# Key and query products of a graph-attention layer: one fp32 product each replaced by three products of rounded high and low parts

## The chip, the cores and the metric

One NeuronCore of one Trainium2 chip runs the whole program in one launch. The metric is device time in microseconds (us) of that launch, lower is better. Beside it stands one execution taken by the hardware profiler; its rows are in us from the start of its span unless marked ns. TensorE's matmuls are PE in the rows and its weight loads PEld; VectorE is DVE, ScalarE ACT, GpSimd POOL, and SP is the engine that only issues DMAs.

## The reference

Two graph layers over 16 batches of 512 nodes with 128 features. The change lies in the second layer; what comes before it is cut.

```python
x = x + _L0_gnn_ref(relu(layernorm(x)), adj, ...)      # eight Euler steps over the graph
h = relu(layernorm(x))
# _L1_gnn_ref, 4 heads of 32:
x1 = relu(layernorm((L_norm @ h) @ Wc + bc) * g1 + be1) + h
q, k, v = x1 @ Wq, x1 @ Wk, x1 @ Wv                     # [512, 128] each, per batch
scores = q @ k.T / sqrt(32), masked by adj > 0
o = softmax(scores) @ v
x2 = layernorm(x1 + o @ Wo + bo) * g2 + be2
out = x + layernorm(x2 + gelu(x2 @ W1 + b1) @ W2 + b2) * g3 + be3
```

## The kernel before

Layer 0 runs up to 419 us; it also takes batch 0 of layer 1 as far as its queries and keys, with helpers of its own calls that the change leaves as they are. Then a block boundary, at which all engines meet, and layer 1.

Layer 1 is written as rounds `r`, unrolled, the same list for every engine. In round `r` batch `r` enters (x1, its turned form x1T, keys, queries, values), batch `r - 1` is attended (scores, softmax, turned probabilities, products with v), and batch `r - 2` leaves (normalisation by the sums, output projection, second layer norm). Batches 1 to 15 enter in rounds 1 to 15. A round has 16 units `u` (4 tiles of 128 query rows by 4 heads). In each unit every engine does its share of the attention and then what the constants `AT_...` put in that unit. Every engine works through its own list strictly in the order of the code; semaphores alone tie the lists together, and an instruction that waits holds up all behind it on its engine.

The share of unit `u` of the batch attended:

- TensorE: `turn` (four 128x128 transposes of an older unit's probabilities, L1767), `scores` of unit `u + 1` (one product of 512 columns, L1754), and in odd units `values` (16 small products, L1787).
- VectorE: the mask and the row minimum of unit `u` (L1935), called mask u below; it writes `prob`. For units 0, 7, 11, 13, 15 it also copies turned probabilities out of PSUM (L1922), three units later.
- ScalarE: the exponential of unit `u` with its sum (L1873), called exp u below, which waits for mask u; the other eleven copies (L1862), also three units later.

What stands around the change in round `r`:

- u = 1, VectorE: `residual` (L340) writes x1 of batch `r`. It waits for `z_norm` (L331) of GpSimd, which was started in the round before.
- u = 2, TensorE: `x1_transpose` (L347) puts x1 turned in PSUM bank 4 (`A_BANK`). ScalarE: `x1T_out` (L354) copies it to `x1T` in SBUF, behind exp 2. VectorE: mask 2, then the copy of unit 15 of the batch before.
- u = 3, TensorE: `k_product` (L359), one fp32 product of 512 columns, which the trace shows as two matmul instructions. ScalarE: `k_hi_out` (L377) writes the rounded high part of k, behind exp 3. VectorE: mask 3, the copy of unit 0, then statistics of the batch that leaves (L285, L291).
- u = 4, TensorE: `q_product` (L363) into bank 4. ScalarE: exp 4, the copy of unit 1, `q_hi_out` (L384), `spread` (L1899). VectorE: mask 4, `k_lo_out` (L389).
- u = 5, VectorE: mask 5, `q_lo_out` (L395), then the standardisation of the batch that leaves (`z_std`, L308).
- u = 6 to 9, TensorE: the graph product of batch `r + 1`, three float32r products a unit (L1829); it waits for `q_lo_ready`, since it uses bank 4 too.
- u = 12, VectorE: `z2` (L1972). GpSimd's `x_bo` (L1711) waits for it, and behind `x_bo` in GpSimd's list stand `rstd_b` (L212), `z_gain` (L327) and `z_norm` (L331) of batch `r + 1`.
- u = 14, TensorE: `v_product` (L368) from `x1T`.

High and low parts: a float32r tile holds a rounded value, the high part is the rounded copy, the low part is the difference to it. The helper `products` pairs high with high, high with low and low with high:

```python
    (left_hi, left_lo), (right_hi, right_lo) = left, right
    return (left_hi, right_hi), (left_hi, right_lo), (left_lo, right_hi)
```

The mask and the exponential in the code:

```python
dve.tensor_tensor_reduce(prob[u % RING][:, :], psum[u % 2][:, :], mask[:, u // HEADS, :], ...).then_inc(masked, 1)
act.wait_ge(masked, UNITS * a + u + 1)
```

Of the kernel before, what the change touches and what calls it, by code (L numbers as in the profile page):

```python
# [18 lines left out]
F32 = mybir.dt.float32  # L19
F32R = mybir.dt.float32r  # L20
BF16 = mybir.dt.bfloat16
ALU = mybir.AluOpType
# [82 lines left out]
def two_layers(nc, x, adj, alpha, w, d, fc_w, fc_b, Wc, bc, g1, be1, Wq, Wk, Wv, Wo, bo, g2, be2, W1, b1, W2, b2,  # L105
# [4 lines left out]
    with ExitStack() as whole:  # L110
# [19 lines left out]
        two_over_lam = tensor(whole, "two_over_lam", [P, 1])  # L130

        one = Shared()
        one.row_in = tensor(whole, "row_in", [1, ROWS, D])
        one.bc_all = tensor(whole, "bc_all", [P, ROWS, D])
        one.Wcs = tensor(whole, "W_c", [P, D])
        one.Wqs = tensor(whole, "W_q", [P, D])
# [11 lines left out]
        one.mean_rstd = tensor(whole, "mean_rstd_a", [P, NT])  # L148
        one.shift = [tensor(whole, f"shift_a{i}", [P, NT]) for i in range(2)]
        one.h = [tensor(whole, f"h{i}", [P, NT, D]) for i in range(2)]  # L150
        one.y, one.Lnorm, one.ident, one.exponent = y, adjT, ident, exponent
        one.dve_waited, one.pool_waited = waited
        one.L_lo = L_lo
# [1258 lines left out]

AT_X1, AT_X1T, AT_X1T_OUT, AT_K, AT_Q, AT_K_HI, AT_Q_HI, AT_K_LO, AT_Q_LO = 1, 2, 2, 3, 4, 3, 4, 4, 5
AT_V, AT_V_OUT = 14, 14
AT_CONV, AT_CONV_OUT, AT_Z, AT_Z_OUT, AT_Z_MOMENTS, AT_Z_STD = 6, 9, 10, 11, 12, 14
AT_Y_MOMENTS, AT_H = 9, (11, 12, 13)
# [24 lines left out]
def layer1(nc, whole, tensor, sem, psum, one, out_dram, y, mask, ident, exponent, waited):  # L1443
# [164 lines left out]
    with ExitStack() as ctx:  # L1608
        def sb(name, shape, dt=F32):
# [2 lines left out]
        stats_c, mv_c = sb("stats_c", [P, NT, 6]), sb("mv_c", [P, NT, 2])  # L1612
        ve_c, rstd_c = sb("ve_c", [P, NT]), sb("rstd_c", [P, NT])
        z2_std = sb("z2_std", [P, NT, D])
        one.x1[1], one.v[1] = sb("x1_1", [P, NT, D]), sb("v_1", [P, NT, D])
        x1 = one.x1
        x1_bo = [sb(f"x1_bo{i}", [P, NT, D]) for i in range(2)]
# [12 lines left out]
        L_parts = (sb("L_hi", [P, NT, N], F32R), one.L_lo)  # L1630
        h_parts = tuple(sb(f"h_{part}", [P, NT, D], F32R) for part in ("hi", "lo"))

        L_hi_ready, L_lo_ready, h_hi_ready, h_lo_ready = (
            sem(n) for n in ("L_hi_ready", "L_lo_ready", "h_hi_ready", "h_lo_ready"))
        z2_std_ready, z2_gain_ready, sums_inv_ready = (
# [40 lines left out]
        with nc.Block() as block:  # L1676
# [12 lines left out]
            def _(pool):  # L1689
# [24 lines left out]
                def round_(r, s, half):  # L1714
                    enters, attends, leaves = parts(r)
                    if leaves:
                        spread_inverses(r - 2)
                    if within(r, 1, BATCH - 2):
                        split_h(r + 1, 1 - s)
                    e = r - 3  # L1720
                    if within(r, 3, BATCH + 2):
                        inverse_root(pool, e, mv_c, c_mv, ve_c, rstd_c, c_pool, z2_std_ready, e, exponent, pool_waited)

                        pool.wait_ge(z2_std_ready, e + 1)
                        pool.tensor_tensor(out=z2_gain[:, :, :], in0=z2_std[:, :, :], in1=all_tiles(one, G2),
                                           op=ALU.mult).then_inc(z2_gain_ready, 1)
                        pool.wait_ge(z2_gain_ready, e + 1)
                        pool.tensor_tensor(out=x2[:, bass.ds(e * N, N)].rearrange("p (t d) -> p t d", d=D),
                                           in0=z2_gain[:, :, :], in1=all_tiles(one, BE2), op=ALU.add
                                           ).then_inc(x2_ready, 1)  # L1730
                    if within(r, 0, BATCH - 3):
                        h_scales(pool, one, r + 2, s)
                    if enters:
                        add_bo(r, s)
                    if within(r, 0, BATCH - 2):
                        z_root(pool, one, r + 1)
                    if within(r, 0, BATCH - 2):
                        norm_z(pool, one, r + 1)
                add_bo(0, 0)
                unrolled(round_, BATCH + 2, first=1)  # L1740
                scales_3(pool, 0)
# [5 lines left out]
            def _(pe):  # L1747
                def scores(a, s, u, half):
                    if u == 0:

                        pe.wait_ge(stacked[s], STACK_DMAS * half)
                    at_least(pe, masked, UNITS * a + u - 1)
                    t, head = divmod(u, HEADS)
                    pe.matmul(psum[u % 2][:, :], q_stack[s][:, head, t * P:(t + 1) * P], k_stack[s][:, head, :],  # L1754
                              start=True, stop=True).then_inc(scores_psum, 1)

                def turn(batch, u):

# [34 lines left out]
                def round_(r, s, half):  # L1793
                    enters, attends, leaves = parts(r)
                    a, e = r - 1, r - 2
                    for u in range(UNITS):
# [19 lines left out]
                            last.then_inc(spread_psum, 1)  # L1816
                        if u == AT_K and enters:
                            at_least(pe, oT_ready, r - 2)
                            k_product(pe, one, psum[7 - s], r)
                        if u == AT_Q and enters:  # L1820
                            q_product(pe, one, A_BANK, r)
                        if AT_CONV <= u < AT_CONV + NT and within(r, 0, BATCH - 2):
                            if u == AT_CONV:
                                pe.wait_ge(q_lo_ready, r + 1)
# [34 lines left out]
            def _(act):  # L1859
# [5 lines left out]
                def round_(r, s, half):  # L1865
                    enters, attends, leaves = parts(r)
                    a, e = r - 1, r - 2
                    for u in range(UNITS):
# [10 lines left out]
                        if x not in DVE_COPIES:  # L1879
                            if u < TURN_LAG and leaves:  # L1880
                                copy_turned(e, x)
                            if u >= TURN_LAG and attends:
                                copy_turned(a, x)
                        if u == AT_X1T_OUT and enters:
                            x1T_out(act, one, A_BANK, r)
                        if u == AT_K_HI and enters:
                            k_hi_out(act, one, psum[7 - s], r, s, half)
# [31 lines left out]
            def _(dve):  # L1919
# [5 lines left out]
                def round_(r, s, half):  # L1925
# [3 lines left out]
                    for u in range(UNITS):  # L1929
# [22 lines left out]
                        if u == AT_RINV and leaves:  # L1952
                            dve.wait_ge(exp_done, UNITS * (e + 1))
                            at_least(dve, rinv_ready, e)
                            dve.reciprocal(sums_inv[:, :], row_sums[s][:, :]).then_inc(sums_inv_ready, 1)
                        if u == AT_K_LO and enters:
                            k_lo_out(dve, one, psum[7 - s], r)
                        if u == AT_Q_LO and enters:
# [70 lines left out]
```

## Time and profile before

| what | value |
|---|---|
| median of 3 runs | 921.42 us (921.39, 921.42, 926.23) |
| profiled execution, its own time | 925.83 us |
| its span, first to last instruction | 924.0 us |
| PE busy | 871.8 us, 94% of the span |
| DVE busy | 650.8 us, 70% |
| ACT busy | 540.9 us, 59% |
| POOL busy | 324.8 us, 35% |
| mean granted TensorE clock | 0.979 |

Matmuls are pipelined and their ends are modelled, so a busy share of PE is not a share of its peak; the distance from one start to the next tells more. Layer 1 with its 15 rounds takes from 419 us to about 812 us; the profiled execution is 4.41 us longer than the median of the three runs.

### The profile page before, as it was taken

How to read it: one execution, taken by the hardware profiler on the slowest of the kernel's cores; microseconds unless marked ns; L12 is line 12 of the kernel's file. 1: busy time of each engine (PE TensorE's matmuls, PEld its weight loads, DVE VectorE, ACT ScalarE, POOL GpSimd, SP SyncE). 2: the span in 40 equal slices, each digit the busy share in tenths (PEclk: the TensorE clock that was granted, in tenths of full speed). 3: DMA queues.
4: the chain of work that ended last, by engine and by line, in shares of the span. 5: the costliest groups of instructions: out<-in, count | busy, mean ns of one | idle time of the engine just before them, and what ended most of it. 6: DMA issues, size and time to landing. Idle time of an engine off the chain costs nothing.

```text
span 924.0 us, 19065 instructions
## 1 busy us (share of the span) xinstructions
PE 871.8 (94%) x6765; PEld 712.7 (77%) x6765; DVE 650.8 (70%) x2110; ACT 540.9 (59%) x1234; POOL 324.8 (35%) x426
## 2 busy tenths in 40 slices
PE   6999999999999999988999999999999999889993
PEld 5779989899999888975777777777777777667772
DVE  6856464644454456536898988888898988887786
ACT  3144342433333323216988888888888887885674
POOL 4111111102020304202354554455555553224776
PEclk9799999999999899999999999999999999999998
DMA  3000000000000000503444455554444545500222
GB/s 100 0 12 13 12 12 12 12 13 12 12 24 1 23 12 1 137 1 105 126 109 98 116 138 139 138 138 111 112 104 106 121 138 138 138 2 1 59 57 69
DMA packets 46428, 61.73 MB, mean 67 GB/s; under 512 B 3567, under 2 KB 21246, under 8 KB 46334
## 3 DMA queue, kind: packets, MB, share of 16 engines
q1 hardware_dynamic: 46034, 60.38, 25.3%
q8 instruction: 55, 0.90, 0.4%
q14 instruction: 39, 0.32, 0.1%
q10 hardware_dynamic: 300, 0.13, 0.1%
HBM read 39.53 MB, written 20.97 MB: 65 GB/s over the span
## 4 chain that ended last, share of the span: by engine, by line
DVE 15%; PE 12%; issue 10%; POOL 9%; ACT 8%; DVEq 0%; POOLq 0%; ACTq 0%
DVE prob L1935 5%; PE bank L1767 4%; PE bank L1787 3%; ACT prob L1873 3%; PE bank L1829 2%; POOL z_gain L327 2%; POOL z_norm L331 2%; ACT probT L1862 2%; DVE z_std L308 2%; POOL x_bo L1711 2%; POOL rstd_b L212 1%; DVE probT L1922 1%; PE bank L1754 1%; POOL rstd L212 1%; DVE stats_c L285 1%
## 5 line engine op out<-in xcount | busy, mean ns | idle before, releaser
L1873 ACT ACTIVATE prob<-prob,low 128x512 f32<-128x512 f32 x256 | 184.0, 719 | 62.9 <-DVE low L1935 61.0
L1935 DVE CUSTOM_DVE_ANT_0 prob<-bank,mask 128x512 f32<-128x512 f32 x256 | 171.0, 682 | 24.2 <-PE bank L1754 22.6
L1767 PE MATMUL bank<-ident,prob 128*128 128x128 f32 x1024 | 161.7, 281 | 13.5 <-ACT probT L1862 13.5
L1767 PEld LDWEIGHTS bank<-ident,prob 128*128 128x128 f32 x1024 | 113.3, 141 | 59.9 <-issue 35.7
L1754 PE MATMUL bank<-k_stack,q_stack 128*128 128x512 f32 x256 | 123.3, 482 | 2.5 <-DVE low L1935 1.4
L820 PE MATMUL bank<-B_hi,halves 128*128 128x384 f32 x384 | 106.4, 339 | 1.6 <-DVE halves L1183 1.1
L1862 ACT ACTIVATE probT<-bank 128x512 f32<-128x512 f32 x176 | 102.6, 583 | 2.6 <-PE bank L1767 1.1
L791 PE MATMUL bank<-halves,P3T_hi 128*128 128x256 f32 x512 | 98.8, 295 | 3.4 <-DVE halves L1201 2.2
L791 PEld LDWEIGHTS bank<-halves,P3T_hi 128*128 128x128 f32 x512 | 84.6, 201 | 5.8 <-DVE halves L1201 2.5
L610 POOL TENSOR_SCALAR var_eps<-mv 128x4 f32<-128x4 f32 x16 | 3.6, 228 | 242.2 <-DVE mv L1127 242.2
L1787 PE MATMUL bank<-probT,v 128*32 128x128 f32 x2048 | 82.3, 279 | 2.7 <-ACT probT L1862 1.1
L1787 PEld LDWEIGHTS bank<-probT,v 128*32 128x32 f32 x2048 | 48.2, 109 | 43.0 <-issue 32.2
L791 PE MATMUL bank<-halves,P3T_lo 128*128 128x256 f32 x256 | 74.6, 291 | 0.0
L820 PEld LDWEIGHTS bank<-B_hi,halves 128*128 128x128 f32 x384 | 70.1, 188 | 4.5 <-DVE halves L1183 2.0
L973 ACT ACTIVATE Sq<-bank,trace_inv 128x512 fp32r<-128x512 f32 x44 | 30.2, 687 | 61.8 <-PE bank L775 61.8
L820 PE MATMUL bank<-B_lo,halves 128*128 128x384 f32 x192 | 64.6, 336 | 0.0
L1922 DVE COPY probT<-bank 128x512 f32<-128x512 f32 x80 | 55.0, 687 | 10.2 <-PE bank L1767 9.5
L964 ACT ACTIVATE halves<-bank 128x512 fp32r<-128x512 f32 x48 | 28.5, 593 | 51.0 <-PE bank L783 51.0
L1193 DVE TENSOR_TENSOR y<-bank,y 128x128 f32<-128x128 f32 x64 | 18.5, 289 | 56.2 <-PE bank L820 46.9
L1183 DVE TENSOR_TENSOR halves<-bank,halves 128x512 fp32r<-128x512 f32 x48 | 33.0, 688 | 33.9 <-ACT halves L964 33.9
L1754 PEld LDWEIGHTS bank<-k_stack,q_stack 128*128 128x128 f32 x256 | 48.7, 191 | 6.9 <-DVE low L1935 5.5
L791 PEld LDWEIGHTS bank<-halves,P3T_lo 128*128 128x128 f32 x256 | 51.4, 201 | 0.0
(263 smaller groups left out, 1963.3 us busy)
## 6 DMA issues: line engine op xcount, KB each, us to landing
k_stack<-bounce_q SPq DMA_DIRECT2D x64, 256.0 KB, 4.8
q_stack<-bounce_k SPq DMA_DIRECT2D x64, 256.0 KB, 7.5
bounce_q<-k_parts SPq DMA_DIRECT2D x16, 512.0 KB, 2.8
bounce_k<-q_parts SPq DMA_DIRECT2D x16, 512.0 KB, 3.1
x_in<-in_x_dram SPq DMA_DIRECT2D x16, 256.0 KB, 2.7
out_dram<-probT SPq DMA_DIRECT2D x16, 256.0 KB, 2.3
y<-in_adj_dram SPq DMA_DIRECT2D x4, 256.0 KB, 3.4
W1s<-in_L_gnn_W_dram SPq DMA_DIRECT2D x1, 128.0 KB, 2.2
```

Source lines behind the costliest of these rows:

```text
L791: last = pe.matmul(psum[2 + nt // 2][:, nt % 2 * 2 * D:(nt % 2 + 1) * 2 * D], power[:, k, nt * P:(nt + 1) * P], c[:, k, :, :].rearrange("p ...
L820: last = pe.matmul(psum[nt % 2][:, 0:GROUP * D], x[:, nt * P:(nt + 1) * P], c[:, m, :, :].rearrange("p i d -> p (i d)"), start=m == 0 and ...
L964: act.activation(T_parts[m][0], psum[4 + m][:, :], ACT.Copy).then_inc(T_hi_ready[m], 1)
L973: act.activation(Sq[1 - s][:, mt, :], SQ_BANK[:, :], ACT.Identity, scale=trace_inv2[:, 0:1], accum_out=v[:, mt:mt + 1]).then_inc(square_re ...
L1183: dve.tensor_tensor(out=T_parts[m][1], in0=psum[4 + m][:, :], in1=T_parts[m][0].bitcast(F32), op=ALU.subtract).then_inc(T_lo_ready[m], 1)
L1754: pe.matmul(psum[u % 2][:, :], q_stack[s][:, head, t * P:(t + 1) * P], k_stack[s][:, head, :], start=True, stop=True).then_inc(scores_psum, 1)
L1767: last = pe.transpose(psum[2 + u % 2][:, mt * P:(mt + 1) * P], prob[u % RING][:, mt * P:(mt + 1) * P], ident[:, :])
L1787: last = pe.matmul(psum[6 + s][rows, t * P:(t + 1) * P], v[s][:, mt, rows], probT[(HEADS * t + head) % TURNED][:, mt, :], start=mt == 0, s ...
L1862: act.activation(probT[u % TURNED][:, :, :].rearrange("p t n -> p (t n)"), psum[2 + u % 2][:, :], ACT.Copy).then_inc(copied_act, 1)
L1873: act.activation(prob[u % RING][:, :], prob[u % RING][:, :], ACT.Exp, bias=low[:, u % TURNED:u % TURNED + 1], scale=-1.0, accum_out=row_su ...
L1922: dve.tensor_copy(probT[u % TURNED][:, :, :].rearrange("p t n -> p (t n)"), psum[2 + u % 2][:, :]).then_inc(copied_dve, 1)
L1935: dve.tensor_tensor_reduce(prob[u % RING][:, :], psum[u % 2][:, :], mask[:, u // HEADS, :], 1.0, 3e38, ALU.add, ALU.min, low[:, u % TURNED ...
```

## The change

The fp32 key and query products of batches 1 to 15 become three float32r products each. At the start of layer 1 GpSimd splits W_k and W_q into high and low parts (four instructions on 128x128). In each round ScalarE writes the high part of x1T in unit 2, into the tile of `q_parts`, which is free by then; VectorE writes the low part in unit 2 (`AT_X1T_LO = 2`), behind the copy of that unit; ScalarE makes the fp32 copy `x1T`, which the value product still reads, in unit 3, once the low part is done. TensorE's key product waits for the low part, and its query product for the fp32 copy, since it writes the bank that both read. A loading buffer, `row_in`, moves into a part of `y` that is not used yet at that time.

```diff
--- before.py
+++ after.py
@@ -130,7 +130,6 @@
         two_over_lam = tensor(whole, "two_over_lam", [P, 1])
 
         one = Shared()
-        one.row_in = tensor(whole, "row_in", [1, ROWS, D])
         one.bc_all = tensor(whole, "bc_all", [P, ROWS, D])
         one.Wcs = tensor(whole, "W_c", [P, D])
         one.Wqs = tensor(whole, "W_q", [P, D])
@@ -148,6 +147,7 @@
         one.mean_rstd = tensor(whole, "mean_rstd_a", [P, NT])
         one.shift = [tensor(whole, f"shift_a{i}", [P, NT]) for i in range(2)]
         one.h = [tensor(whole, f"h{i}", [P, NT, D]) for i in range(2)]
+        one.row_in = y[0:1, 12 * N:12 * N + ROWS * D].rearrange("o (r d) -> o r d", d=D)
         one.y, one.Lnorm, one.ident, one.exponent = y, adjT, ident, exponent
         one.dve_waited, one.pool_waited = waited
         one.L_lo = L_lo
@@ -1412,7 +1412,7 @@
 
 
 
-AT_X1, AT_X1T, AT_X1T_OUT, AT_K, AT_Q, AT_K_HI, AT_Q_HI, AT_K_LO, AT_Q_LO = 1, 2, 2, 3, 4, 3, 4, 4, 5
+AT_X1, AT_X1T, AT_X1T_OUT, AT_X1T_LO, AT_K, AT_Q, AT_K_HI, AT_Q_HI, AT_K_LO, AT_Q_LO = 1, 2, 2, 2, 3, 4, 3, 4, 4, 5
 AT_V, AT_V_OUT = 14, 14
 AT_CONV, AT_CONV_OUT, AT_Z, AT_Z_OUT, AT_Z_MOMENTS, AT_Z_STD = 6, 9, 10, 11, 12, 14
 AT_Y_MOMENTS, AT_H = 9, (11, 12, 13)
@@ -1612,6 +1612,8 @@
         stats_c, mv_c = sb("stats_c", [P, NT, 6]), sb("mv_c", [P, NT, 2])
         ve_c, rstd_c = sb("ve_c", [P, NT]), sb("rstd_c", [P, NT])
         z2_std = sb("z2_std", [P, NT, D])
+        x1T_parts = tuple(one.q_parts[:, part, :] for part in range(2))
+        Wk_parts, Wq_parts = (tuple(sb(f"{n}_{part}", [P, D], F32R) for part in ("hi", "lo")) for n in ("W_k", "W_q"))
         one.x1[1], one.v[1] = sb("x1_1", [P, NT, D]), sb("v_1", [P, NT, D])
         x1 = one.x1
         x1_bo = [sb(f"x1_bo{i}", [P, NT, D]) for i in range(2)]
@@ -1630,6 +1632,7 @@
         L_parts = (sb("L_hi", [P, NT, N], F32R), one.L_lo)
         h_parts = tuple(sb(f"h_{part}", [P, NT, D], F32R) for part in ("hi", "lo"))
 
+        x1T_hi_ready, x1T_lo_ready, W_split = sem("x1T_hi_ready"), sem("x1T_lo_ready"), sem("W_split")
         L_hi_ready, L_lo_ready, h_hi_ready, h_lo_ready = (
             sem(n) for n in ("L_hi_ready", "L_lo_ready", "h_hi_ready", "h_lo_ready"))
         z2_std_ready, z2_gain_ready, sums_inv_ready = (
@@ -1736,6 +1739,12 @@
                         z_root(pool, one, r + 1)
                     if within(r, 0, BATCH - 2):
                         norm_z(pool, one, r + 1)
+                pool.wait_ge(one.weights_loaded, 16 * 5)
+                for n, (source, (hi, lo)) in enumerate(((one.Wks, Wk_parts), (one.Wqs, Wq_parts))):
+                    pool.tensor_copy(hi[:, :], source[:, :]).then_inc(W_split, 1)
+                    pool.wait_ge(W_split, 2 * n + 1)
+                    pool.tensor_tensor(out=lo[:, :], in0=source[:, :], in1=hi[:, :].bitcast(F32),
+                                       op=ALU.subtract).then_inc(W_split, 1)
                 add_bo(0, 0)
                 unrolled(round_, BATCH + 2, first=1)
                 scales_3(pool, 0)
@@ -1753,6 +1762,11 @@
                     t, head = divmod(u, HEADS)
                     pe.matmul(psum[u % 2][:, :], q_stack[s][:, head, t * P:(t + 1) * P], k_stack[s][:, head, :],
                               start=True, stop=True).then_inc(scores_psum, 1)
+
+                def split_product(pe, bank, parts):
+                    for n, (w, x) in enumerate(products(parts, x1T_parts)):
+                        last = pe.matmul(bank[:, :], w[:, :], x, start=n == 0, stop=n == 2)
+                    return last
 
                 def turn(batch, u):
 
@@ -1816,9 +1830,12 @@
                             last.then_inc(spread_psum, 1)
                         if u == AT_K and enters:
                             at_least(pe, oT_ready, r - 2)
-                            k_product(pe, one, psum[7 - s], r)
+                            pe.wait_ge(W_split, 4)
+                            pe.wait_ge(x1T_lo_ready, r)
+                            split_product(pe, psum[7 - s], Wk_parts).then_inc(one.k_psum, 1)
                         if u == AT_Q and enters:
-                            q_product(pe, one, A_BANK, r)
+                            pe.wait_ge(x1T_ready, r + 1)
+                            split_product(pe, A_BANK, Wq_parts).then_inc(one.q_psum, 1)
                         if AT_CONV <= u < AT_CONV + NT and within(r, 0, BATCH - 2):
                             if u == AT_CONV:
                                 pe.wait_ge(q_lo_ready, r + 1)
@@ -1882,6 +1899,11 @@
                             if u >= TURN_LAG and attends:
                                 copy_turned(a, x)
                         if u == AT_X1T_OUT and enters:
+                            act.wait_ge(one.x1T_psum, r + 1)
+                            act.wait_ge(one.q_written[1 - s], 16 * (half + s))
+                            act.activation(x1T_parts[0], A_BANK[:, :], ACT.Copy).then_inc(x1T_hi_ready, 1)
+                        if u == AT_K_HI and enters:
+                            act.wait_ge(x1T_lo_ready, r)
                             x1T_out(act, one, A_BANK, r)
                         if u == AT_K_HI and enters:
                             k_hi_out(act, one, psum[7 - s], r, s, half)
@@ -1953,6 +1975,11 @@
                             dve.wait_ge(exp_done, UNITS * (e + 1))
                             at_least(dve, rinv_ready, e)
                             dve.reciprocal(sums_inv[:, :], row_sums[s][:, :]).then_inc(sums_inv_ready, 1)
+                        if u == AT_X1T_LO and enters:
+                            dve.wait_ge(x1T_hi_ready, r)
+                            dve.tensor_tensor(out=x1T_parts[1], in0=A_BANK[:, :],
+                                              in1=x1T_parts[0].bitcast(F32), op=ALU.subtract
+                                              ).then_inc(x1T_lo_ready, 1)
                         if u == AT_K_LO and enters:
                             k_lo_out(dve, one, psum[7 - s], r)
                         if u == AT_Q_LO and enters:
```

## Rows read from the trace of the kernel before

**Rows 1.** The page, part 1: busy us, share of the span, instructions.
```profile
PE 871.8 (94%) x6765; PEld 712.7 (77%) x6765; DVE 650.8 (70%) x2110; ACT 540.9 (59%) x1234; POOL 324.8 (35%) x426
```

**Rows 2.** Busy us by window, one round: length, PE, PEld, DVE, ACT, POOL; clock.
```profile
604.00:630.00 26.00, 25.20 (x256) 18.67 (x256) 23.07 (x77) 22.06 (x54) 13.37 (x17) 1.00 0.49 123
```

**Rows 3.** Chain of waits through round 8: start, us, what was last.
```profile
603.77 0.29 DVE x L340
...
610.44 0.59 ACT q_parts L384
...
611.67 1.11 DVE z_std L308 x4
...
622.19 0.70 DVE z L1972
...
629.88 0.30 DVE x L340
```

**Rows 4.** Timeline of VectorE, units 2 to 9 of that round.
```profile
605.37 0.68 DVE L1922 COPY probT<-bank 128x512 f32<-128x512 f32 x1
...
605.97 0.67 DVE L1935 CUSTOM_DVE_ANT_0 prob<-bank,mask 128x512 f32<-128x512 f32 x1
...
608.51 0.69 DVE L1935 CUSTOM_DVE_ANT_0 prob<-bank,mask 128x512 f32<-128x512 f32 x1
...
609.13 0.69 DVE L389 TENSOR_TENSOR k_parts<-bank,k_parts 128x512 fp32r<-128x512 f32 x1
...
609.73 0.68 DVE L1935 CUSTOM_DVE_ANT_0 prob<-bank,mask 128x512 f32<-128x512 f32 x1
...
611.06 0.69 DVE L395 SCALAR_TENSOR_TENSOR q_parts<-bank,q_parts 128x512 fp32r<-128x512 f32 x1 [0.64 <-ACT q_parts L384]
...
616.45 0.69 DVE L1935 CUSTOM_DVE_ANT_0 prob<-bank,mask 128x512 f32<-128x512 f32 x1 [1.00 <-PE bank L1754]
```

**Rows 5.** Timeline of ScalarE, units 2 to 4 of that round.
```profile
605.48 0.72 ACT L1873 ACTIVATE prob<-prob,low 128x512 f32<-128x512 f32 x1 [0.24 <-DVE low L1935]
...
606.20 0.58 ACT L354 ACTIVATE x1T<-bank 128x512 f32<-128x512 f32 x1
...
608.06 0.60 ACT L377 ACTIVATE k_parts<-bank 128x512 fp32r<-128x512 f32 x1 [0.55 <-PE bank L359]
...
609.24 0.72 ACT L1873 ACTIVATE prob<-prob,low 128x512 f32<-128x512 f32 x1 [0.59 <-DVE low L1935]
```

**Rows 6.** Timeline of TensorE, units 3 to 6 of that round.
```profile
606.92 1.10 PE L359 MATMUL bank<-x1T,W_k 128*128 128x512 f32 x2
...
607.95 0.64 PE L1787 MATMUL bank<-probT,v 128*32 128x128 f32 x16
...
609.26 1.02 PE L363 MATMUL bank<-x1T,W_q 128*128 128x512 f32 x2
...
610.11 0.60 PE L1767 MATMUL bank<-ident,prob 128*128 128x128 f32 x4
...
612.19 0.39 PE L1829 MATMUL bank<-L_hi,h_hi 128*128 128x512 f32 x1
...
612.42 0.40 PE L1829 MATMUL bank<-L_lo,h_hi 128*128 128x512 f32 x1
```

**Rows 7.** Timeline at the start of layer 1, round 1.
```profile
419.71 1.28 POOL L1711 TENSOR_TENSOR x_bo<-x,bc_all 128x512 f32<-128x512 f32 x1 [34.15 <-POOLq L564]
...
421.63 1.62 POOL L1696 TENSOR_TENSOR h_lo<-h,h_hi 128x512 fp32r<-128x512 f32 x1
...
425.38 1.12 PE L359 MATMUL bank<-x1T,W_k 128*128 128x512 f32 x2 [0.84 <-ACT x1T L354]
...
426.39 0.68 DVE L1935 CUSTOM_DVE_ANT_0 prob<-bank,mask 128x512 f32<-128x512 f32 x1
...
430.89 0.50 PE L1829 MATMUL bank<-L_hi,h_hi 128*128 128x512 f32 x1 [0.26 <-DVE q_parts L395]
```

**Rows 8.** Chain of waits in round 2.
```profile
450.64 1.06 PE bank L359 x2
```

## The prediction

> **What bounds the kernel now.** I read the page first, then the busy time of one round, then the chain of waits, and last the timeline of that round around the change. The page makes TensorE look like the bound, busy 94% of the span [rows 1], and in a round it is 25.20 of 26.00 us [rows 2]. But its matmuls overlap each other in the records, and the weight loads fill only 18.67 us. VectorE is busy 23.07 us and ScalarE 22.06 [rows 2]. No engine is full, so the order of the work decides, and that is what the chain of waits shows [rows 3].
>
> Follow round 8. It starts with `residual` on VectorE at 603.77, runs over `q_hi` on ScalarE at 610.44 and `z_std` at 611.67 to z2 at 622.19, then through GpSimd's list to z_norm, and the next residual starts at 629.88 [rows 3]: 26.11 us, the length of a round. The chain is a loop, since the residual of a round needs z_norm from the round before, and GpSimd makes that only after z2. What is lost between residual and z2 on the chain lengthens every round.
>
> The change acts in units 2 to 5, and there the reader should look at VectorE [rows 4]. The copy of unit 2 starts at 605.37, mask 3 at 605.97, mask 4 at 608.51, `k_lo` at 609.13, mask 5 at 609.73; none of them has a wait in its row, VectorE goes through its list without a pause. The one wait is that of `q_lo` for ScalarE, 0.64 us. Yet that wait hangs on VectorE too: ScalarE's exp 4 waited 0.59 us for mask 4 [rows 5], and behind exp 4 stand the copy of unit 1 and `q_hi`. So mask 3, mask 4, exp 4, `q_hi`, `q_lo`, `z_std` form one string that starts when mask 3 starts. TensorE stands beside it: behind the key product it goes on at 607.95 [rows 6], and nobody on the string waits for that.
>
> **The change, part by part.**
>
> *The products.* TensorE spends 1.03 us on the key product (606.92 to 607.95) and 0.85 on the query product (609.26 to 610.11) [rows 6]. The three float32r products of 512 columns in unit 6 follow each other by 0.23 us (612.19, 612.42) [rows 6], so each triple takes 0.69. The change removes 0.34 + 0.16 = 0.50 us a round on TensorE. In rounds 3 to 15 I count this as nothing, since TensorE is not on the string there; were it, it would be 15 x 0.50 = 7.5 us.
>
> *The high part.* It takes the place of the old copy, same engine, same bank, same shape: 606.20 to 606.78 [rows 5]. It can't start earlier, because it is behind exp 2, which starts at 605.48 after mask 2 [rows 5]. Cost nothing.
>
> *The low part.* One VectorE instruction like `k_lo`: 0.69 us from PSUM and SBUF [rows 4], and the next starts 0.60 after its start (609.13 to 609.73). It stands in unit 2 ahead of mask 3, and it waits for the high part. VectorE is done with its copy at 606.05 and then holds until 606.78. A VectorE instruction starts about 0.03 after the ScalarE one it waits for (`q_lo` at 611.06 [rows 4], behind a `q_hi` from 610.44 to 611.03 [rows 3]), so the low part starts at 606.81 and mask 3 at 607.41 instead of 605.97 [rows 4]: 1.44 us later, of which 0.60 is work and 0.84 is the wait. Queued behind the low part are mask 3, the copy of unit 0, the statistics, mask 4; waiting for these are exp 3 and exp 4, then the string above. It has no slack, so I take the whole 1.44 a round. The lower bound is 0.60, the work alone, if the wait were recovered further on.
>
> *The fp32 copy in unit 3.* One more ScalarE copy of 0.58 [rows 5], behind exp 3 and ahead of `k_hi` and exp 4. Exp 3 now follows mask 3 at about 608.1 and is over by 609.0; the copy then ends at 609.5, `k_hi` at 610.0. Mask 4 is now at 608.51 + 1.44 = 609.95, so exp 4 comes at 609.24 + 1.44 = 610.68 at the earliest. About 0.7 us cover is left, so the copy costs nothing in rounds 3 to 15; without that cover it would cost up to 0.58.
>
> *The new waits on TensorE.* The key product waits for the low part, until 607.5 instead of starting at 606.92 [rows 6], and is over at 608.2; the products with v behind it come 0.3 later than 607.95, turned tiles too. The query product waits for the fp32 copy, 609.5 against 609.26. Both shifts are smaller than the 1.44 of the string, so they don't set it.
>
> *Splitting the weights.* Four GpSimd instructions of 128x128 at the head of its list. The row nearest to them is a 128x512 addition, 1.28 us [rows 7]; a quarter of it each is 1.3 us, whole ones would be 5.1. Behind them stand x_bo of batch 0 and the parts of h, whose last one ends at 423.25; the graph product needs these at 430.89, and the key product of round 1 starts at 425.38 [rows 7]. Even 5.1 us from 419.71 ends at 424.8. Cost nothing. The moved loading buffer adds no transfer and no wait: nothing.
>
> *Rounds 1 and 2* differ. In round 1 VectorE comes late to mask 3 (426.39) anyway, for another splitting; the low part finds its high part ready and pushes mask 3 by 0.60 only. ScalarE is late there too, and the fp32 copy adds up to 0.58 to `q_hi`, so the graph product at 430.89 [rows 7] comes about 1.1 later (0.6 to 1.4). In round 2 the key product itself is on the chain [rows 8]: it starts some 0.65 later (0.69 + 0.03 less what it waited already), the triples give 0.50 back, and the fp32 copy of 0.58 comes ahead of a ScalarE that has no slack in this round; I take 0.6 (0.2 to 1.4).
>
> *Sum.* 13 rounds x 1.44 = 18.7, plus 1.1 and 0.6: 20.4 us. The profiled execution would go from 925.83 to 946.2. It is 4.41 us above the median of the three runs; the addition is the same for both, so the median goes from 921.42 to 941.8, I say **942**.
>
> One reading of the page decides whether TensorE's saving counts at all. By its busy share in the round, 25.20 us, it would be the bound, and the sum would be -7.5 us; by VectorE's 23.07 of 26.00 the change adds to the fullest engine [rows 2]. The Trainium skill's page Perfetto Trace Analysis, section Identifying the Most-Contended Engine, says that the busy share of matmuls is a poor measure since they are pipelined, that weight loads are a better one, and that occupancy is fair for VectorE. By that rule VectorE is the most contended engine and this change loads it further, which speaks against it; the trace agrees with the order (18.67 against 23.07).
>
> **The rivals.**
>
> *Only VectorE's own work counts.* The 0.84 us of waiting come back, because VectorE idles further on: mask 9 waits 1.00 us for TensorE at 616.45 [rows 4]. Then 15 x 0.60 = 9.0, 930.4 us. For it: 2.9 us of idle VectorE in the round. Against it: the scores that mask 9 waits for hang on exp 6 and a copy behind `z_std`, so they move with the string.
>
> *It all fits into idle time:* 921.4. VectorE's 2.9 us idle are more than the 1.44. The same objection, doubly.
>
> *TensorE is the bound after all:* -7.5 us, 913.9, faster. It decides if VectorE and ScalarE could take up the 1.44 and the chain ran over the matmuls from unit 2 to unit 9. In round 2 it does run over the key product [rows 8]; in the later rounds VectorE's rows without a wait speak against it.
>
> *The fp32 copy is on the path too,* because `k_hi` or the copies behind it come late: 13 x (1.44 + 0.58) = 26.3, plus 2.8 at the upper values of rounds 1 and 2, 29.1: 950.5.
>
> **How the numbers follow.** Forecast as worked out 0.70 (its own range 938 to 949, from 0.1 us a round either way, and from the 4.41 us between the runs shown); VectorE's work alone 0.11; fits into idle time 0.05; TensorE the bound 0.06; copy on the path too 0.08. The range of 929 to 951 holds the first two and the last. A measurement of this kernel tells about 0.5% (4.6 us) from no change. Faster 0.06, same 0.06 (idle time, and a little of the second case), slower 0.88.
>
> **What would show it.** Right: residual to residual is 27.5 us instead of 26.1 in rounds 3 to 15; VectorE's low part shows a wait of about 0.8 for ScalarE; mask 3 starts 3.6 after the residual, not 2.2; `z_std` about 9.3 after it, not 7.9; z2 to the next residual stays at 7.7. The triples take 0.69 each, and VectorE's busy time in a round grows by 0.69 only. Wrong: the round is 26.1 and mask 9 no longer waits; or the low part starts without a wait; or ScalarE's exp 4 starts directly behind `k_hi`. The granted clock of 1.00 in the round [rows 2] stood with waits of up to 1.00 us; a lower one around the key product's new wait would add time that I haven't counted.

## The result: 948.84 us against 921.40

The changed kernel takes 948.84 us (median of 4 runs, 946.68 to 949.96), the kernel before 921.40 beside it (4 runs, 921.39 to 926.23). The ratio is 1.0278, interval 1.0242 to 1.0313: slower, by 27.4 us from median to median. The profiled execution took 949.61 us (span 947.8, granted clock 0.974) against 925.83 (span 924.0, 0.979): 23.8 us more.

The page of the changed kernel, part 1 (busy us, share of the span, instructions), answers to [rows 1]:

```profile
PE 875.9 (92%) x6795; PEld 720.7 (76%) x6795; DVE 663.4 (70%) x2125; ACT 547.5 (58%) x1249; POOL 326.4 (34%) x430
```

VectorE and ScalarE have 15 instructions more each, one a round, and TensorE's busy share fell. Nothing here looks like 24 us. The windows show one round, from residual to residual, as in [rows 2]:

```profile
586.24:613.81 27.57, 25.47 (x259) 19.12 (x258) 24.02 (x78) 22.61 (x55) 13.46 (x17) 1.00 0.48 116
```

The round takes 27.57 us instead of 26.11 [rows 3], at the same full clock. The cause stands in the timeline of VectorE, units 2 to 9 of the next round; its residual starts at 613.81. It answers to [rows 4]:

```profile
613.81 1.07 DVE L340 SCALAR_TENSOR_TENSOR x<-z_norm,h 128x512 f32<-128x512 f32 x1
...
615.40 0.68 DVE L1944 COPY probT<-bank 128x512 f32<-128x512 f32 x1
...
616.85 0.69 DVE L1980 TENSOR_TENSOR q_parts<-bank,q_parts 128x512 fp32r<-128x512 f32 x1 [0.76 <-ACT q_parts L1904]
...
617.46 0.68 DVE L1957 CUSTOM_DVE_ANT_0 prob<-bank,mask 128x512 f32<-128x512 f32 x1
...
620.00 0.69 DVE L1957 CUSTOM_DVE_ANT_0 prob<-bank,mask 128x512 f32<-128x512 f32 x1
...
622.55 0.69 DVE L395 SCALAR_TENSOR_TENSOR q_parts<-bank,q_parts 128x512 fp32r<-128x512 f32 x1 [0.64 <-ACT q_parts L384]
...
623.16 1.11 DVE L308 TENSOR_SCALAR z_std<-z,mv_c,rstd_c 128x128 f32<-128x128 f32 x4
...
627.95 0.69 DVE L1957 CUSTOM_DVE_ANT_0 prob<-bank,mask 128x512 f32<-128x512 f32 x1 [0.99 <-PE bank L1763]
```

The low part (L1980) stands between the copy and mask 3. VectorE is done with the copy at 616.08, holds 0.76 us for ScalarE's high part, and starts mask 3 at 617.46, 3.65 us after the residual instead of 2.20 [rows 3, 4]. Mask 4, `q_lo` and `z_std` come later by the same amount: `z_std` 9.35 after the residual instead of 7.90 [rows 3]. The idle time of mask 9 is still 0.99, so VectorE recovers nothing there.

On ScalarE exp 4 waits for mask 4, with the fp32 copy (L354) and `k_hi` well before it; on TensorE the key product waits 0.75 us for the low part. ScalarE, units 3 and 4, as in [rows 5]:

```profile
618.90 0.57 ACT L354 ACTIVATE x1T<-bank 128x512 f32<-128x512 f32 x1
...
619.38 0.59 ACT L377 ACTIVATE k_parts<-bank 128x512 fp32r<-128x512 f32 x1
...
620.73 0.72 ACT L1890 ACTIVATE prob<-prob,low 128x512 f32<-128x512 f32 x1 [0.77 <-DVE low L1957]
```

The chain of waits through round 3 of the changed kernel, up to the next residual, in the columns of [rows 3]:

```profile
476.00 0.29 DVE x L340
...
478.53 0.49 ACT q_parts L1904
...
479.65 0.68 DVE prob L1957
...
485.33 1.11 DVE z_std L308 x4
...
495.85 0.70 DVE z L1999
```

From z2 (495.85) to the next residual (503.54 in the timeline) it is 7.69 us, the 7.7 of before. So the length was added between residual and z2. Between exp 4 and `z_std` the profile leads this chain over the copy of unit 1 and its turn and scores on TensorE. By the code `z_std` does not wait for scores, and the timeline above has `z_std` (623.16) right behind `q_lo` (622.55), which waited for `q_hi`: the string that was forecast.

From the starts of the residuals, the 23.8 us of the two profiled executions divide like this:

| stretch | before | after | more | forecast |
|---|---|---|---|---|
| start to first residual | 421.32 | 421.38 | 0.06 | 0 |
| round 1 | 26.19 | 28.39 | 2.20 | 1.1 |
| round 2 | 25.79 | 26.23 | 0.44 | 0.6 |
| rounds 3 to 14 | 313.51 | 331.37 | 17.86 | 17.3 |
| residual of round 15 to the end | 137.19 | 140.43 | 3.24 | 1.4 |

### The profile page after: what moved, and what is told of

It reads as the page before. It is cut to its first block, busy times and chain, and to the rows that moved or that the text cites. A ratio compares the mean times of both kernels' runs of the same rounds, so it can differ in the third digit from the quotient of the medians.

```text
span 947.8 us, 19176 instructions
## 1 busy us (share of the span) xinstructions
PE 875.9 (92%) x6795; PEld 720.7 (76%) x6795; DVE 663.4 (70%) x2125; ACT 547.5 (58%) x1249; POOL 326.4 (34%) x430
## 4 chain that ended last, share of the span: by engine, by line
DVE 15%; PE 13%; issue 11%; POOL 10%; ACT 7%; DVEq 0%; POOLq 0%; ACTq 0%
PE bank L1781 5%; DVE prob L1957 4%; PE bank L1801 2%; ACT prob L1890 2%; PE bank L1846 2%; POOL z_gain L327 2%; POOL z_norm L331 2%; ACT probT L1879 2%; DVE z_std L308 2%; POOL x_bo L1714 2%; POOL rstd_b L212 2%; PE bank L1763 2%; DVE probT L1944 1%; POOL rstd L212 1%; DVE stats_c L285 1%
```

## The experiments

The main theory: VectorE's list carries the loop, and the low part costs it 0.6 of work and 0.84 of wait each round. The rivals: ScalarE's second copy, the products themselves, TensorE as the bound. "Before" is in each case the kernel before on the same chip.

**The wait alone.** The low part moves one unit back, behind mask 3 and the copy of unit 0.

```diff
-..., AT_X1T_OUT, AT_X1T_LO, AT_K, ... = ..., 2, 2, 3, ...
+..., AT_X1T_OUT, AT_X1T_LO, AT_K, ... = ..., 2, 3, 3, ...
```

> The changed kernel with the low part one unit later on VectorE, behind mask 3 and the copy of unit 0. By then the high part is ready, so the wait of 0.8 us goes and its work of 0.60 stays; the key product starts about 0.4 us later still. Theory (VectorE's string from mask 3 to z_std sets the round): a round of 26.7 us instead of 27.56 in the changed kernel and 26.10 in the kernel before, some 11 us less than the changed kernel. Rival (the key product that waits for the low part sets the round): not under 27.56, time as the changed kernel or longer. Rival (only work counts, waits don't): 27.56 too, since the work is the same.

935.56 us (4 runs), ratio 1.0135 (1.0112 to 1.0157); a round is 26.74. VectorE's timeline in that kernel has the low part without a wait:

```profile
609.66 0.68 DVE L1980 TENSOR_TENSOR q_parts<-bank,q_parts 128x512 fp32r<-128x512 f32 x1
```

So 27.56 - 26.74 = 0.82 of the round was the wait; 0.64 over before's 26.10 is left. The key product waits longer here, 1.09 instead of 0.75, and the round is shorter all the same, so the key product does not set it:

```profile
610.49 0.71 PE L1768 MATMUL bank<-q_parts,W_k_hi 128*128 128x512 f32 x2 [1.09 <-DVE q_parts L1980]
```

Round 1 became longer, 30.04 instead of 28.39.

**The work alone.** Without the low part: the high part stands in for it in the products, which wait for the high part. This leaves the low half of x1 out of keys and queries.

```diff
-                    for n, (w, x) in enumerate(products(parts, x1T_parts)):
+                    for n, (w, x) in enumerate(products(parts, (x1T_parts[0], x1T_parts[0]))):
...
-                        if u == AT_X1T_LO and enters:
-                            dve.wait_ge(x1T_hi_ready, r)
-                            dve.tensor_tensor(out=x1T_parts[1], in0=A_BANK[:, :],
...
```

> The changed kernel without the low part of x1 turned: the products use the high part in its place, so the low half of x1 is left out of keys and queries, and the number of products is the same. Key product and fp32 copy wait for the high part only. Theory: the round falls back to 26.10 us, that of the kernel before, though TensorE still has its triples and ScalarE its second copy; time about 2 us above the kernel before, from round 1. Rival (TensorE's triples or the second ScalarE copy are part of the loss): a round between 26.4 and 27.5. Rival (TensorE is the bound and its 0.50 us a round count once the low part is out of the way): 25.6, some 6 us under the kernel before.

925.96 us (9 runs), ratio 1.0036 (1.0018 to 1.0054); a round is 26.10, that of before. The triples, the high part and the fp32 copy are all in it, and neither lengthen nor shorten a steady round. From profile to profile it is 1.0 us more than before, as round 1 takes 27.23 instead of 26.19.

**The low part in the kernel before.** The fp32 products and the single ScalarE copy stay; VectorE gets the instruction with its wait in unit 2, and the key product waits for it.

```diff
+                        if u == AT_X1T_LO and enters:
+                            dve.wait_ge(one.q_written[1 - s], 16 * (half + s))
+                            dve.wait_ge(x1T_ready, r + 1)
+                            dve.tensor_tensor(out=one.q_parts[:, 1, :], in0=A_BANK[:, :],
+                                              in1=one.x1T[:, :], op=ALU.subtract
+                                              ).then_inc(x1T_lo_ready, 1)
...
```

> The kernel before with the low part's instruction alone, in unit 2 ahead of mask 3 and with its wait for ScalarE's copy; keys and queries stay single fp32 products, which wait for the low part too, and there is one ScalarE copy. (The low part is the bank less its own fp32 copy, and nothing reads it.) Theory: a round of 27.56 us in rounds 3 to 15, as in the changed kernel, so that the products and the second copy there are worth nothing. Rival (the products' 0.50 us a round do count): 28.06. Rival (the second ScalarE copy is part of the loss): under 27.4.

946.24 us (4 runs), ratio 1.0242 (1.0211 to 1.0273); a round is 27.63, round 1 28.14. One instruction with its wait does nearly all that the whole change does. These three experiments pin the steady round from both sides: 26.10 without the low part, 27.63 with it alone.

**Is TensorE near?** The kernel before with one copy less on VectorE: that of unit 0 goes to ScalarE.

```diff
-DVE_COPIES = (0, 7, 11, 13, 15)
+DVE_COPIES = (7, 11, 13, 15)
```

> The kernel before, with one thing moved: the copy of unit 0's turned probabilities goes from VectorE to ScalarE (unit 3, between exp 3 and k_hi, where ScalarE waits for the key product). Theory (VectorE's string sets the round): mask 4 and all behind it come 0.60 us earlier, a round of 25.5 instead of 26.10, some 8 us under the kernel before. Rival (TensorE sets the round): 26.1 and no change. Rival (ScalarE has no room): k_hi comes late, exp 4 with it, and the gain is under 0.2 us a round.

919.84 us (10 runs), ratio 0.9975 (0.9959 to 0.9991); a round is 25.98. VectorE was relieved of 0.60 and the round gave 0.12: the theory in its simple form missed. The chain of waits of this kernel shows why:

```profile
601.66 1.10 PE bank L359 x2
...
604.14 0.87 PE bank L363 x2
...
605.04 0.61 ACT q_parts L384
...
606.28 0.88 DVE z_std L308 x4
```

It now runs over TensorE's matmuls from unit 0 through the key and the query product to `q_hi`, and on to `z_std` as before. TensorE's string was some 0.1 us behind VectorE's. The other rival, ScalarE without room, had a gain of under 0.2 too, but `q_hi` waits for TensorE, so ScalarE had 0.36 us to spare there:

```profile
605.04 0.60 ACT L384 ACTIVATE q_parts<-bank 128x512 fp32r<-128x512 f32 x1 [0.36 <-PE bank L363]
```

**The weights' split.** The four GpSimd instructions move from the head of layer 1 to the end of GpSimd's list in layer 0.

```diff
+                for n, (source, (hi, lo)) in enumerate(((one.Wks, one.Wk_parts), (one.Wqs, one.Wq_parts))):
+                    pool.tensor_copy(hi[:, :], source[:, :]).then_inc(one.W_split, 1)
...
-                for n, (source, (hi, lo)) in enumerate(((one.Wks, Wk_parts), (one.Wqs, Wq_parts))):
-                    pool.tensor_copy(hi[:, :], source[:, :]).then_inc(W_split, 1)
...
```

> The changed kernel with the weights split at the end of layer 0, where GpSimd idles for 34 us, not at the start of layer 1. Theory (in round 1 the split pushes GpSimd's x_bo and the parts of h under two VectorE instructions that have both inputs in SBUF): residual of round 1 back from 1.78 to 0.79 us, the low part of L from 2.89 to 2.29, and round 1 from 28.39 to about 28.1, as in the run with the low part alone; rounds 3 to 15 stay at 27.56. Rival (the split is hidden, the stretched instructions have another cause): both durations stay.

945.98 us (4 runs), ratio 1.0258 (1.0229 to 1.0287); round 1 is 27.74 instead of 28.39 (about 28.1 was expected), the later steady ones 27.55. The rows are shown in the next section.

**Two moves in the kernel before.** The copy of unit 0 goes to ScalarE, and `z_std`, which is ready earlier, goes ahead of `q_lo` and its wait.

```diff
-DVE_COPIES = (0, 7, 11, 13, 15)
+DVE_COPIES = (7, 11, 13, 15)
...
+                        if u == AT_Z2_STD and finishes:
+                            dve.wait_ge(c_pool, 2 * f + 2)
+                            at_least(dve, z2_gain_ready, f)
+                            standardise(dve, z2_std, z2, mv_c, rstd_c, z2_std_ready)
                         if u == AT_Q_LO and enters:
...
```

> The kernel before with copy 0 on ScalarE as in the earlier run, and with z_std of the batch that leaves moved ahead of q_lo on VectorE, so that VectorE no longer idles 0.6 us for q_hi with z_std ready behind it. Theory (after the first move TensorE runs without a pause to the query product, and the string goes q_hi, q_lo, z_std, mask 6): mask 6 comes 0.6 earlier, of which the products in units 6 and 7 let 0.4 through; a round of 25.6 instead of 25.98, some 10 us under the kernel before. Rival (TensorE alone sets the round by now): 25.9 or more. Rival (the graph product, which waits for q_lo, now comes late and eats it up): 26.0 or more.

916.42 us (6 runs), ratio 0.9929 (0.9911 to 0.9948): 0.7% less than the kernel before. A round is 25.65, and its chain stays on TensorE from 598.02 to 613.93.

**The same two moves in the changed kernel,** with the low part in unit 3.

```diff
-..., AT_X1T_OUT, AT_X1T_LO, AT_K, ... = ..., 2, 2, 3, ...
+..., AT_X1T_OUT, AT_X1T_LO, AT_K, ... = ..., 2, 3, 3, ...
...
-DVE_COPIES = (0, 7, 11, 13, 15)
+DVE_COPIES = (7, 11, 13, 15)
...
+                        if u == AT_Z2_STD and finishes:
...
```

> The changed kernel with the low part in unit 3, copy 0 on ScalarE and z_std ahead of q_lo: the same two moves as the run beside it, with the products in parts. Theory (the low part's 0.60 us on VectorE is only partly given back by TensorE's 0.50): a round of 25.85, 0.3 above the run beside it, and about 3 us more in rounds 1 and 2. Rival (once TensorE sets the round the triples win): 25.3 to 25.5. Rival (ScalarE, with three copies behind exp 3, sets it): 26.2 or more.

925.88 us (10 runs), ratio 1.0040 (1.0025 to 1.0055); a round is 26.17, not 25.85. The row of the key product tells what is left:

```profile
607.32 0.70 PE L1768 MATMUL bank<-q_parts,W_k_hi 128*128 128x512 f32 x2 [0.73 <-DVE q_parts L1980]
```

TensorE itself now waits 0.73 us a round for the low part, more than the triples save. The number of the ScalarE rival, 26.2, came out, but not its mechanism: exp 4 waits 0.28 us for mask 4 there, and the chain of waits runs from the low part (606.49) to the key product and stays on TensorE up to 619.21.

**Without the low part and with copy 0 on ScalarE** (the low half of x1 left out as above): does the second ScalarE copy cost something then?

```diff
-DVE_COPIES = (0, 7, 11, 13, 15)
+DVE_COPIES = (7, 11, 13, 15)
...
-                        if u == AT_X1T_LO and enters:
...
```

> The changed kernel without the low part (the high part used in its place, so the low half of x1 is left out of keys and queries) and with copy 0 on ScalarE. The kernel before with copy 0 moved has 25.98 us a round, with its key and query products on the chain; here they are triples. Theory (TensorE's saving counts only where VectorE is out of the way): about 25.75, since ScalarE's second copy takes back half of the 0.50. Rival (TensorE's saving counts in full): 25.5. Rival (it counts for nothing): 25.98 or more.

918.83 us (10 runs), ratio 0.9959 (0.9944 to 0.9974); a round is 25.71, 0.27 below the 25.98 of the kernel before with the same copy moved. The chain of waits runs over the fp32 copy on ScalarE; how much of the round that copy costs was not tried alone.

```profile
607.43 0.48 ACT x1T L354
...
609.46 0.62 ACT q_parts L384
```

**The bound for the triples:** the same with `z_std` ahead of `q_lo`, so that a free low part, a relieved VectorE and the float32r products meet (the low half of x1 left out again).

```diff
-DVE_COPIES = (0, 7, 11, 13, 15)
+DVE_COPIES = (7, 11, 13, 15)
...
-                        if u == AT_X1T_LO and enters:
...
+                        if u == AT_Z2_STD and finishes:
...
```

> The changed kernel without the low part (the high part used in its place, so the low half of x1 is left out of keys and queries) with both moves: copy 0 on ScalarE, z_std ahead of q_lo. It bounds what the triples could bring if the low part cost nothing; the kernel before with both moves has 25.65 us a round, set by TensorE from unit 0 to unit 9. Theory (there TensorE's 0.50 us count, and the wait of z_std for q_hi behind ScalarE's second copy is gone): 25.2 to 25.3. Rival (ScalarE's second copy sets the round by now): 25.6 or more, so that the triples could not pay even with a free low part.

915.68 us (5 runs), ratio 0.9939 (0.9908 to 0.9969); a round is 25.56, only 0.09 below the two moves alone, not 0.35 to 0.45. The chains of both kernels run over TensorE at the same place. First this one, then that of the two moves in the kernel before:

```profile
602.00 0.94 PE bank L1768 x3
...
604.33 0.69 PE bank L1768 x3
...
607.08 0.92 PE bank L1846 x3
```

```profile
601.83 1.10 PE bank L359 x2
...
604.33 0.86 PE bank L363 x2
...
607.25 0.69 PE bank L1829 x3
```

The triples save 0.16 and 0.17 on the chain, and the first graph product takes 0.23 more. VectorE's `q_lo`, behind `z_std` by the second move, ran from 606.31 to 606.99 here, and the graph product, which may not touch the bank earlier, starts behind it:

```profile
606.31 0.68 DVE L395 SCALAR_TENSOR_TENSOR q_parts<-bank,q_parts 128x512 fp32r<-128x512 f32 x1
...
607.05 0.50 PE L1846 MATMUL bank<-L_hi,h_hi 128*128 128x512 f32 x1
```

What the products give, the wait for `q_lo` takes back for the most part. That is read from the rows; no run took that wait away.

## Why the prediction was right, and which terms were off

*The direction and the mechanism held.* The forecast was 1.44 us a round from the low part on VectorE, 0.60 work and 0.84 wait. Measured: 27.56 - 26.10 = 1.46 a round, of which moving the instruction back gave 0.82 and leaving it out 0.64 more. Mask 3 at 3.6 and `z_std` at 9.3 after the residual, the wait of about 0.8 and the unchanged 7.7 behind z2 were all found. VectorE's busy time went from 23.17 and 23.18 in rounds 7 and 8 of the kernel before to 23.86 and 23.87 in the two rounds of the changed one ahead of the window shown (24.02): the 0.69 that was forecast. The total alone would not have told this: 948.84 stands at the upper edge of the forecast's own range, 938 to 949, and nearer to the 950.5 of the last rival, the fp32 copy on the path too, than to 942. That rival needs some 28.1 us a round, and the rounds have 27.56.

*TensorE's saving counted as nothing:* right in this kernel, but by little. TensorE's own string runs only some 0.1 us behind VectorE's, and with one copy less on VectorE its matmuls are the chain. And the saving needs x1T split first, which stands ahead of the key product on the same chain. With the low part free, 0.27 a round is left after one move (25.98 to 25.71) and 0.09 after both (25.65 to 25.56).

The saving itself was mis-sized, 0.50 a round. From start to start the key triple takes 0.87, not 0.69, and the query triple 0.70. In unit 3 a product takes some 0.17 longer than in unit 4, the fp32 one too (1.03 against 0.85); the forecast had that in the fp32 product and not in the triple. So it is 0.16 + 0.15, close to the chains above (0.16 + 0.17), and 15 rounds would give some 5 us instead of 7.5:

```profile
617.68 0.70 PE L1768 MATMUL bank<-q_parts,W_k_hi 128*128 128x512 f32 x2 [0.75 <-DVE q_parts L1980]
...
618.55 0.65 PE L1801 MATMUL bank<-probT,v 128*32 128x128 f32 x16
...
619.85 0.63 PE L1768 MATMUL bank<-q_parts,W_q_hi 128*128 128x512 f32 x2
...
620.55 0.60 PE L1781 MATMUL bank<-ident,prob 128*128 128x128 f32 x4
```

The 25.2 to 25.3 expected of the last experiment had counted the 0.50 too.

*The fp32 copy hidden in unit 3:* right in this kernel; exp 4 waited 0.77 for mask 4 behind it, the cover of 0.7 that was worked out. It holds only while VectorE is late: with the low part out and VectorE relieved the copy is on the chain.

*Splitting the weights, "cost nothing":* this step failed. The four instructions took 1.6 us, within the bounds, and nobody waited for their result. What was not asked is whom the instructions pushed behind them run beside. VectorE's residual and its L_lo, round 1 of the changed kernel:

```profile
421.38 1.78 DVE L340 SCALAR_TENSOR_TENSOR x<-z_norm,h 128x512 f32<-128x512 f32 x1
...
424.25 2.89 DVE L1962 TENSOR_TENSOR L_lo<-adjT,L_hi 128x2048 fp32r<-128x2048 f32 x1 [0.47 <-ACT L_hi L1894]
```

and with the split moved into layer 0:

```profile
421.69 0.69 DVE L343 SCALAR_TENSOR_TENSOR x<-z_norm,h 128x512 f32<-128x512 f32 x1
...
424.55 2.29 DVE L1965 TENSOR_TENSOR L_lo<-adjT,L_hi 128x2048 fp32r<-128x2048 f32 x1 [1.57 <-ACT L_hi L1897]
```

From the start of the residual to the end of L_lo it is 5.76 us in the one and 5.15 in the other, 0.61 less, and the round is 0.65 shorter. With the split left at the head of layer 1 and the low part left out, the two rows are 1.78 and 2.89 again.

*Round 1, 2.20 instead of 1.1.* Besides that, the low part is behind L_lo, and the key product waited 2.27 for it. The windows give a granted clock of 0.50, the 1.2 GHz level, in that stretch, where before's was 0.96, and the matmul rows behind the wait are long (the transposes 1.05, where before's took 0.60 at 426.35):

```profile
424.00:429.00 5.00, 2.73 (x10) 2.06 (x9) 4.75 (x6) 2.02 (x5) 0.98 (x1) 0.50 0.00 0
```

```profile
427.88 1.19 PE L1768 MATMUL bank<-q_parts,W_k_hi 128*128 128x512 f32 x2 [2.27 <-DVE q_parts L1980]
...
429.30 1.05 PE L1781 MATMUL bank<-ident,prob 128*128 128x128 f32 x4
```

The prediction had named a lower clock around that wait as time not counted. But this wait did not bring the clock down: it is at 0.50 from 421 us on in both kernels. In the kernel before it is back at 1.00 by 425, in the changed kernel only by 432 (by 428 without the low part). First the changed kernel, then the kernel before:

```profile
425.00:431.00 6.00, 3.73 (x11) 2.67 (x11) 5.24 (x9) 3.02 (x8) 0.00 (x0) 0.50 0.00 0
```

```profile
425.00:431.00 6.00, 4.57 (x20) 2.64 (x21) 5.44 (x11) 4.22 (x11) 0.00 (x0) 1.00 0.16 64
```

With the split moved and with the low part alone the clock was at 1.00 from 425 to 427 and at 0.50 from 429 to 431, behind waits of the key product of 2.77 and 2.63. How the rest of the 2.20 divides between the wait and the clock was not tried. In the steady round shown the key product's wait is 0.75 and the clock 1.00.

*Round 15 and the tail, 3.24 instead of 1.44.* The extra 1.8 is not the string. With the split moved, a kernel that is otherwise equal, residual to end took 138.9, 1.7 over before and close to the forecast. The clock differs too: in windows of 10 us up to 935 the changed kernel has two at 0.83 (815 to 825 and 885 to 895), the kernel before one (855 to 865), the kernel with the split moved none. The window from 815 to 825 of the changed kernel, then that with the split moved:

```profile
815.00:825.00 10.00, 7.65 (x76) 5.47 (x73) 6.40 (x19) 8.51 (x22) 2.76 (x3) 0.83 0.90 236
```

```profile
815.00:825.00 10.00, 7.37 (x78) 5.42 (x82) 7.98 (x22) 8.94 (x23) 2.55 (x2) 1.00 0.97 249
```

TensorE had waited 1.30 and then 0.83 us there for turned probabilities (before's rows at that place show 0.51 and 0.84); the transposes behind that took 1.11 instead of 0.66:

```profile
817.89 0.63 PE L1781 MATMUL bank<-ident,prob 128*128 128x128 f32 x4 [1.30 <-ACT probT L1879]
...
819.81 0.64 PE L1801 MATMUL bank<-probT,v 128*32 128x128 f32 x16 [0.83 <-ACT probT L1879]
...
820.38 1.11 PE L1781 MATMUL bank<-ident,prob 128*128 128x128 f32 x4
```

With the split moved, the same two waits stand there, 1.30 and 0.83, and the clock stayed up behind them. With the low part alone they are 1.28 and 0.83, and the window has 0.83 again. So the longer wait goes with the low part in unit 2 (0.39 with it in unit 3), the lower clock with some executions of it; what decides between them stays open. Of the four runs of the changed kernel, the two with a mean clock of 0.974 took 949.61 and 949.96, those with 0.980 and 0.978 took 946.68 and 948.07.

*From profile to median.* The forecast took the 20.4 us over to the median unchanged; profile to profile it was 23.8, median to median 27.4. The first residual of layer 1 comes at 421.3 to 421.7 in six of the eleven profiled executions, those of both kernels among them, and at 416.2 to 418.1 in the other five. Before's median lies 4.4 below its profiled execution, after's 0.8 below its own. The runs without a profile have no trace, but their mean granted clocks are on record. Of 49 runs of the kernel before beside the experiments, 37 took 920.3 to 923.0 at a clock of 0.983 to 0.988, and twelve took 923.4 to 928.1 at 0.976 to 0.982. Its profiled execution, 0.979, is like the twelve. The changed kernel's four runs have 0.974 to 0.980, some of which comes from round 1 and the tail. So the forecast's step from profile to median, the same addition for both, went from one of before's rarer executions to its common ones. This points to where the last 3.6 us come from, but does not show it.

## What to carry to other kernels

Before adding an instruction to a list that runs in order, find the string that closes the loop and ask whether it passes through that place: here 0.69 us of work on an engine with 2.9 us idle in a round cost 1.46, more than half of it for where it stood and what it waited for. A saving on the fullest-looking engine is worth what is left when its preparation stands on the same string; measure that bound with the preparation left out before building it. Move work that is ready ahead of instructions that wait: such a move, with one copy taken off the loaded list and no new arithmetic, gave 0.9929 of the time before.

## What the runs showed of the hardware

Who starts first decides what an overlap of GpSimd and VectorE costs, in the few rows there are. In the changed kernel the residual, two inputs in SBUF, starts 0.05 us behind GpSimd's x_bo (421.33) and takes 1.78 us; L_lo, also two inputs in SBUF, starts under GpSimd's h_lo (423.71 to 424.98) and takes 2.89 instead of 2.29. With the split moved, the residual starts 0.01 us ahead of h_lo and takes 0.69, and it is h_lo that becomes longer, 1.81 instead of 1.27. The Trainium skill has both in SBUF — State Buffer, section Who interferes with whom: a VectorE instruction with two SBUF inputs contends with a GpSimd instruction that reads SBUF, and the order of issue decides who blocks. The trace agrees, and these numbers are the price here.

In layer 0, before any of the edits but the moved split can act, the granted clock in 300 to 340 us was 0.87 in the six executions whose layer 1 began late and 0.96 in the five where it began early (the low part in unit 3, one copy less, the two moves in both kernels, the bound for the triples). That goes with the 3 to 5.5 us between the two starts. Both groups hold kernels with and without the change, and an edit in layer 1 has no way to it that a trace showed.

A few steady rounds took 0.3 us longer, 27.85 for the one whose VectorE timeline stands under the result. There VectorE's second statistics instruction waited 0.54 for the first, where such rows have 0.17; why was not tried:

```profile
635.69 0.38 DVE L291 BATCH_NORM_AGGREGATE mv_b<-stats_b 128x2 f32<-128x6 f32 x4 [0.54 <-DVE stats_b L285]
```
